# Running sums over sorted edges in a four-layer graph kernel: one-hot products replaced by scans over turned rows, and a straight-line GpSimd program

## The reference

```python
edge_index = jnp.stack([src, dst])
h = jnp.maximum(_layernorm(x), 0.0)
# GCN: segment sum by src of edge_weight * (h @ W)[dst]
x = x + segment_sum(edge_weight[:, None] * (h @ W)[dst], src) + bias
h = jnp.maximum(_layernorm(x), 0.0)
# GAT: x1 = leaky(h) @ W1.T + b1; hg = x1 @ Wg.T; 4 heads
alpha = leaky(a_src[src] + a_dst[dst], 0.2)          # per edge and head
coeff = softmax of alpha over the edges of one dst
x = x + leaky(segment_sum(hg[src] * coeff, dst) + bias_g, 0.01) @ W2.T + b2
h = jnp.maximum(_layernorm(x), 0.0)
# hypergraph: node -> hyperedge -> node
he = segment_sum((h * d_v_inv_sqrt)[src], dst_clipped) * (hw / d_e)
x = x + (segment_sum(he[dst_clipped], src) * d_v_inv_sqrt) @ W.T + b
h = jnp.maximum(_layernorm(x), 0.0)
# tensor product: weights per edge from a small network on edge_attr
mid = segment_sum(edge_features(h[src] @ w1, w(edge)), dst)   # 256 wide
x = x + linear(mid)
```

## Time and profile before

| what | value |
|---|---|
| median of 3 runs | 3786.72 us |
| lowest, highest | 3783.6, 3790.44 us |
| span of the profiled execution (its own time) | 4093.3 us |
| PE, PE weight loads | busy 48%, 37% of the span |
| DVE | 44% |
| ACT | 25% |
| POOL (GpSimd) | 68% |
| DMA, mean | 105 GB/s |

### The profile page before, as it was taken

One profiled execution on the slowest core, in us unless ns is written; L12 is line 12 of the kernel. 1 busy time (PEld: TensorE's weight loads), 2 busy tenths in 40 slices (PEclk: granted clock), 3 DMA queues, 4 the chain that ended last, 5 costly groups with the idle time before them and its releaser, 6 DMA issues.

```text
span 4093.3 us, 41473 instructions
## 1 busy us (share of the span) xinstructions
PE 1958.2 (48%) x8810; PEld 1502.6 (37%) x8810; DVE 1792.4 (44%) x5891; ACT 1029.1 (25%) x2706; POOL 2776.5 (68%) x2522
## 2 busy tenths in 40 slices
PE   0010002247731656557499923346666662216774
PEld 0000001135521444445377723334444441215773
DVE  2974301158831333233655426663333321207894
ACT  0000000134521444445011114442222221003442
POOL 0828876678886555553288876647888887667887
PEclk9999995567765666667555555555555555557997
DMA  3969813356652111111255434445555554437885
GB/s 86 307 116 332 282 36 97 95 116 106 109 84 46 39 39 42 39 39 25 41 69 69 62 58 116 120 112 104 102 102 102 95 98 99 115 101 156 171 171 104
DMA packets 469349, 430.13 MB, mean 105 GB/s; under 512 B 121817, under 2 KB 377975, under 8 KB 468979
## 3 DMA queue, kind: packets, MB, share of 16 engines
q0 software_dynamic: 156800, 133.81, 23.0%
q1 hardware_dynamic: 258098, 236.96, 18.5%
q10 hardware_dynamic: 54404, 58.86, 5.9%
HBM read 227.32 MB, written 148.92 MB: 92 GB/s over the span
## 4 chain that ended last, share of the span: by engine, by line
POOL 19%; issue 13%; DMA 6%; PE 4%; SPq 4%; DVE 2%; another core or an unknown queue 1%; ACT 1%; POOLq 0%; ACTq 0%; DVEq 0%
POOL out_dram L655 14%; POOL work L641 5%; DMA out_dram<-work 3%; DMA work<-big 2%; PE bank L806 1%; SPq L511 1%; PE bank L910 1%; PE bank L909 1%; SPq L504 1%; DMA work<-keys_clip 1%; POOL work L608 1%; ACT work L1124 1%; SPq L528 0%; SPq L145 0%
## 5 line engine op out<-in xcount | busy, mean ns | idle before, releaser
L655 POOL DMA_INDIRECT out_dram<-work x784 | 1258.5, 1605 | 268.2 <-issue 199.8
L641 POOL DMA_INDIRECT work<-out_dram,work x980 | 942.0, 961 | 613.1 <-issue 413.6
L806 PE MATMUL bank<-work 128*128 128x128 f32 x1568 | 378.1, 417 | 680.2 <-issue 316.4
L806 PEld LDWEIGHTS bank<-work 128*128 128x128 f32 x1568 | 334.1, 313 | 727.4 <-issue 568.4
L1669 DVE SCALAR_TENSOR_TENSOR work<-work,bank 128x128 f32<-128x128 f32 x975 | 320.5, 345 | 319.3 <-PE bank L806 183.3
L1124 ACT ACTIVATE work<-work 128x128 f32<-128x128 f32 x784 | 316.7, 480 | 128.7 <-issue 55.3
L641 POOL DMA_INDIRECT work<-rec_d,work x196 | 216.6, 1105 | 53.4 <-issue 46.7
L1652 DVE TENSOR_TENSOR work<-work 128x512 f32<-128x512 f32 x245 | 168.3, 687 | 175.7 <-DMA work<-keys_src 70.3
L641 POOL DMA_INDIRECT work<-he,work x196 | 199.9, 1020 | 53.6 <-issue 46.2
L853 PE MATMUL bank<-work,w_W1T 128*128 128x512 f32 x196 | 151.5, 917 | 118.0 <-ACT work L1187 108.9
L1117 ACT ACTIVATE work<-work,eps_col 128x4 f32<-128x4 f32 (+1 forms) x196 | 59.0, 301 | 549.1 <-issue 289.7
(11 more groups left out here) (281 smaller groups left out, 4400.5 us busy)
## 6 DMA issues: line engine op xcount, KB each, us to landing
out_dram<-big SPq DMA_DIRECT2D x71, 726.0 KB
big<-in_x_dram SPq DMA_DIRECT2D x71, 704.0 KB
work<-big SPq DMA_DIRECT2D x98, 264.0 KB
edge_w<-big SPq DMA_DIRECT2D x49, 512.0 KB
work<-edge_w ACTq DMA_DIRECT2D x49, 512.0 KB
work<-out_dram,work POOLq DMA_INDIRECT x980
big<-work SPq DMA_DIRECT2D x49, 264.0 KB
work<-keys_src ACTq DMA_DIRECT2D x49, 256.5 KB
```

The source lines that it names most:

```text
L641: g_.indirect_dma_start(ring_[G.place][:, k * columns:(k + 1) * columns], None, table_ap, bass.IndirectOffsetOnAxis(ap=idx_r[G.place][:, k ...
L655: g_.indirect_dma_start(table[:, :], bass.IndirectOffsetOnAxis(ap=idxa_r[G.place][:, k:k + 1], axis=0), ring_[G.place][:, k * ROW:(k + 1) ...
L806: last = T.matmul(out[:, t * P:(t + 1) * P], lhs[:, t * P:(t + 1) * P], rhs[:, t * P:(t + 1) * P], start=True, stop=True)
```

## The change

**Sums.** The one-hot product and the carry chain go. A flag per edge (1 where its key equals the key before it) is made once in stage 1 for each of the three key lists and stored in device memory; the key columns `key_col` for `clip` and `src` and the stored list `keys_clip` go. In each sum stage SP broadcasts 512 flags per group into a ring of 4 (`load_flags`), PE only transposes the rows (`turn_tiles`), and DVE makes one running scan over 512 edges per bank, state = flag * state + row, with the last column of the group before as its start. In GCN the transposing product has the edge weights on its diagonal (`diag`, made by ACT from `ident`).

**GpSimd.** All loops are written out (`every_group`); the gathers and adds take their indices from the index arrays where they lie; no index copies and no index DMAs. In GCN and TP the gathers write into `big` and the adds read from it; SP's copies, `big_in` and `fed` go. A gather of group G in these stages waits for the gathers of G-4 (`rows_in`), an add for `kept` of its group and the adds of G-4.

**GAT.** W1 and Wg, and W1 and the attention vectors, are multiplied together once in stage 1 (`WF`, `attF`, with the constant parts `bF4`, `att_c`); the steps `first` and `bias` go, and the buffers behind `turn` and `project` are doubled.

**HYP on DVE** is written in plain order (front, scan, scale), where before the carry chain was interleaved by hand with the statistics. `key_col` copies and a memset ahead of TP go; about 13 small DVE instructions and 4 matmuls are added to the preparation of the weights in stage 1.

```diff
-        def load_keys(eng, G, which, S):
-            if G.from_(2):
-                eng.wait_ge(S["sel"], G.g - 1)
-            k = keys_dram[which]
...
-            eng.dma_start(keys_r[G.slot][:, 0:GE + 1], part.partition_broadcast(P)).then_inc(keys_at.of(G), 16)
+        def load_flags(eng, G, which, S):
+            if G.from_(UNROLL):
+                eng.wait_ge(S["chained"], G.g - (UNROLL - 1))
+            k = flags_dram[which]
...
+            eng.dma_start(flag_r[G.place], part.partition_broadcast(P)).then_inc(flags_at.of(G), 16)
@@ SP
-            move_rows("GCN", GCN, ROW, idx["dst_s"], idx["add_s"])
+            for_groups(sp, lambda G: load_flags(sp, G, "src", GCN))
             stage_end(sp, 2)
-            for_groups(sp, lambda G: load_indices(G, "GAT", [idx["src_d"], idx["dst_d"]]))
...
-            move_rows("TP", TP, D, idx["src_d"], idx["add_d"])
+            for_groups(sp, lambda G: load_flags(sp, G, "dst", TP))
@@ GpSimd
             def gathers(name, table_ap, of, free=None, columns=ROW, ring_=rows_r, done_before=0):
-                def move(G):
+                def body(G):
                     if G.from_(UNROLL):
                         if free is None:
-                            big_in.wait(pool, name, G.before(UNROLL))
+                            rows_in.wait(pool, name, G.before(UNROLL))
                         else:
                             pool.wait_ge(free, G.g + (done_before - UNROLL + 1))
...
+                    for j, f in enumerate(of):
+                        for t in range(GROUP):
+                            k, at_ = j * GROUP + t, G.g * GROUP + t
+                            to = (big[:, at_ * ROW:(at_ + 1) * ROW] if free is None
+                                  else ring_[G.place][:, k * columns:(k + 1) * columns])
+                            g_.indirect_dma_start(to, None, table_ap,
+                                                  bass.IndirectOffsetOnAxis(ap=f[:, at_:at_ + 1], axis=0)
...
+            def adds(name, of, ready, ring_=None):
+                def body(G):
+                    pool.wait_ge(ready, G.g + 1)
+                    if G.from_(UNROLL):
+                        added.wait(pool, name, G.before(UNROLL))
...
+            def every_group(body):
+                for g in range(NG):
+                    body(group(g))
@@ PE
-            def sum_tiles(G, S, rhs, lhs, out, ready):
...
+            def turn_tiles(G, S, of, out):
+                if G.from_(2):
+                    pe.wait_ge(S["chained"], G.g - 1)
                 for t in range(GROUP):
+                    last = T.transpose(out[:, t * P:(t + 1) * P], of[:, t * P:(t + 1) * P], ident[:, :])
                 return last
@@ PE, GAT
+            def project(G):
...
+                T.matmul(b[:, :], one[0:1, :], bF4[0:1, :], start=True, stop=False)
                 for t in range(GROUP):
+                    T.matmul(b[:, t * P:(t + 1) * P], x_[:, t * P:(t + 1) * P], wts["WF"][:, :],
+                             start=False, stop=t == GROUP - 1)
@@ DVE
-            def carry_on(G, banks, ring_, t, k):
...
+            def run_scan(G, to, before, of, rows=slice(0, P)):
+                return V.tensor_tensor_scan(to, flag_r[G.place][rows, :], of, before if G.from_(1) else 0.0,
+                                            ALU.mult, ALU.add)
+            def chain(G, S, name, banks, ring_, free):
+                flags_at.wait(dve, name, G)
+                dve.wait_ge(S["turned"], G.g + 1)
                 if G.from_(2):
                     dve.wait_ge(S[free], G.g - 1)
+                if G.from_(1):
+                    dve.wait_ge(S["chained"], G.g)
+                for k, b in enumerate(banks):
+                    o = 512 * k
+                    ins = run_scan(G, ring_[G.slot][:, o:o + 512], ring_[1 - G.slot][:, o + 511:o + 512], b[:, :])
                 ins.then_inc(S["chained"], 1)
```

More of the change, by code:

```diff
@@ L313, in build_gnn @@
         added = Slots([sem(f"added{k}") for k in range(UNROLL)], [("GCN", 64), ("GATSUM", 64), ("HYPSUM", 64), ("TP", 64)])
[L314 to L321, removed]
+        flags_at = Slots([sem(f"flags_at{k}") for k in range(UNROLL)],
+                         [("GCN", 16), ("GATSUM", 16), ("HYP", 16), ("HYPSUM", 16), ("TP", 16)])
         def ring(start, size, n=2, dt=fp32):
@@ L871, in body @@
                 if G.from_(1):
-                    second(G.before())
-                first(G)
+                    project(G.before())
             for_groups(pe, body)
-            second(group(NG - 1))
+            project(group(NG - 1))
             stage_end(pe, 3)
@@ L934, in body, with turn @@
             def body(G):
[L935 removed]
+                turn(G)
                 if G.from_(1):
[L937 removed]
+                    back(G.before())
             for_groups(pe, body)
[L939 removed]
+            back(group(NG - 1))
             stage_end(pe, 6)
[L943 removed]
+            def turn(G):
                 rows_in.wait(pe, "HYPSUM", G)
[L945 removed]
+                turn_tiles(G, HYPSUM, rows_r[G.place], bank[G.slot]).then_inc(HYPSUM["turned"], 1)
             def delta(G):
@@ L1126, in norm @@
                 last.then_inc(S["h"], 1)
-            def next_keys(G, which, S):
-                if not (isinstance(G.g, int) and G.g == NG - 1):
-                    load_keys(act, G.after(), which, S)
             def keep(G):
@@ L1167, in keep @@
                 act.wait_ge(GAT["hh"], G.g + 1)
-                S_.copy(cols4(big, G, 512), bank[4][:, :]).then_inc(GAT["kept"], 1)
-            def bias(G):
-                act.wait_ge(GAT["xx"], G.g + 1)
-                for k in range(2):
-                    last = S_.activation(xxT8[:, k * 512:(k + 1) * 512], bank[2 + k][:, :], ACT.Identity, bias=cols[:, 0:1])
-                last.then_inc(GAT["xxs"], 1)
+                S_.copy(cols4(big, G, 512), bank[4 + G.slot][:, :]).then_inc(GAT["kept"], 1)
             def body(G):
@@ new lines, in front @@
+            def front(G):
+                rows_in.wait(dve, "HYP", G)
+                if G.from_(2):
+                    dve.wait_ge(HYP["turned"], G.g - 1)
+                r = rows_r[G.place].rearrange("p (t c) -> p t c", c=ROW)
+                V.tensor_tensor(t4(v_r[G.slot]), r[:, :, 0:D], over(wts["K2"][:, :], GROUP), ALU.subtract
+                                ).then_inc(HYP["taken"], 1)
+                dve.wait_ge(HYP["taken"], G.g + 1)
+                statistics(G, HYP, lambda t: v_r[G.slot][:, t * P:(t + 1) * P], GROUP)
```

453 lines of the change are left out of this document (150 added, 303 removed).

## The result

The changed kernel takes 3816.1 us (median of 4 runs, 3815.4 to 3817.0), the kernel before beside it 3785.2 us: a ratio of 1.0078, with a 95% interval of 1.0061 to 1.0096. It is slower by 31 us where 104 us less were forecast. In some groups of runs the kernel before takes 3785 us and in others 4054 to 4099 us, for reasons that stay open, so each ratio here is formed inside one group, and stage times are compared inside one kind of group.

What follows compares the result with a forecast made beforehand. POOL's issue without a gap was taken to bound every stage of an undisturbed execution. The terms -15 - 14 - 23 - 12 - 7 - 8 - 12 - 4 + 1 - 10 = -104 took 3787 to 3683 us; 8-in-10 range 3500 to 3745.

Steps and rivals of the forecast that it cites:

- Preparation: Stage 1: seventeen small DVE and PE instructions, three flag comparisons and stores, less index copies; +4 - 3 = +1 us.
- The choice of the basis: All terms taken against 3786.7 us, reading 304 us of POOL stalls as belonging to the profiled execution only.
- The first rival: Stalls where gathers run also exist in undisturbed executions, and the change cuts their chains: 3511 us, chance 0.15.
- Index copies in GATSUM: GATSUM's adds: without index copies in POOL's stream, adds at 1.595 us take 371.4 us in all; -15 us.
- HYP: HYP stage: gathers at 247 us, -14 us; separately its tail from 31.1 to 19 us, -12 us.
- GATSUM's first wait and GAT's tail: GATSUM's first add after 11 us instead of 18.67, -8; GAT's last group loses one product and one ACT pass, -4.
- Turns: GCN and TP, gathers to adds: without SP's copies the first add waits 4 us instead of 8.62 and 11.33; -12 us.
- Starts: Starts of GAT, GCN and TP: the index transfer behind the barrier goes, half of 5.03 us each; -7 us.
- Slots that DVE lengthens: POOL's gathers and adds lengthened by DVE's masks and carries: -10 us, bounds 0 and -42.
- Written-out loops: GpSimd's loops: 0.7 us for 10 jumps back in GCN's adds, so nothing to gain and nothing taken.
- At nothing, DVE's HYP body: DVE bodies counted as nothing, covered by POOL's issue, 5.0 us per group of gathers; the text names GCN's and TP's.
- The slower rival: Adds and gathers reading rows and indices in place make POOL's slots 0.146 us dearer: 3998 us, chance 0.06.

Runs made afterwards that it cites:

- Run 2: Kernel before with only a wait added: ACT takes no records until a DVE comparison behind its dense pass; 4216.8 against 4054.5 us, 1.039.
- run 3: Changed kernel again, 3815.5 us (1.0076), and beside it with the src flags' store behind the record copying, 3662.2 us (0.9672); before 3785.7.
- run 1: Changed kernel with ACT's store of the src flags moved behind the record copying, in a slower group; 3935.2 us against 4054.5 of before, 0.970.
- the moved store: Changed kernel with ACT's src flag store swapped behind the copying of records; 3935.2 us in a slower group, 3662.2 in a faster one.
- run 5: Kernel before with GpSimd's loops written out, indices read in place, no index copies or index DMAs; 3989.5 against 4054.5 us, 0.9843.
- run 6: As run 5, with GCN and TP gathering into the big buffer and SP's row copies gone; 3972.1 against 4054.5 us of before, 0.9792.
- its third run: Kernel of run 6 measured again in a slower group; 4002.8 us beside 4097.1 of before, 0.9772.
- run 7: The moved store with two two-input comparisons of 128x512 per group put back on DVE in all five sum stages; 3752.6 us, 90 more.
- run 8: The moved store with each scan of 128x512 made twice, one input in SBUF and one in PSUM; 3710.4 us, 48 more.

## Why the prediction was wrong

**The step that failed** is *Preparation*, priced at +1 us with its "three flag comparisons and stores"; it cost about 153. I counted what the stores cost and not what the third waits for. It stands in ACT's stream ahead of the copying of records, which it holds for DVE's whole dense pass. Run 2 gives the wait alone at 162 us, run 3 its removal at 153. The stage table shows it in one piece (434.7 against 282.6). The order of the instructions on ACT was to be had before the run; I looked at GpSimd's and DVE's alone.

**The choice of the basis** had a wrong reason, and did little harm. I took the 304 us of stalls for a thing of profiling, because they came to the same as the 306.6 us between span and median. But profiling does not make them: in run 1 the profiled execution took 3945.5 us with a span of 3943.3, in a group whose median is 3935.2, and its trace has them. They belong to the groups where before takes 4054 to 4099 us, and the 4093.3 us of the profiled execution of before lie among these. That before has none of them where it takes 3785 us is not shown, since no trace of it comes from such a group; the changed kernel has none there. In the timeline of the moved store in a slower group (run 1), GAT:

```profile
1545.71 1.95 PE L775 MATMUL bank<-ident,work 128*128 128x128 f32 x8
...
1559.04 1.07 ACT L1104 COPY work<-bank 128x512 f32<-128x512 f32 x2 [7.82 <-remote]
```

ACT copies the result of eight transposes 11 us after the end that the record gives them, as in the earlier trace rows. In the faster groups GAT's gathers take 490 to 492 us without a gap, 392 x 1.25, and in the slower ones 592 to 650. GCN shows it most. The windows from its first gather to its last, of the moved store in a slower group (run 1) and in a faster one (run 3), in the columns of the earlier trace rows:

```profile
575.40:828.50 253.10, 25.32 (x112) 20.96 (x112) 18.84 (x69) 16.16 (x46) 192.47 (x196) 0.56 0.25 59
...
578.20:824.60 246.40, 171.30 (x886) 133.82 (x887) 138.86 (x444) 106.45 (x319) 186.91 (x196) 0.74 0.36 88
```

In the slower one PE does 112 of its products beside the gathers, in the faster 886, in the same kernel; the rest is left for the adds. The first rival took the stalls for real and expected 82 + 112 us of them to be saved with the rest; in the slower groups the change without its wait gains 119 us (run 1), against 123.5 in the faster, and runs 5 and 6 show why it is no more: the stalls move from the gathers to the adds behind them. What makes the other engines late stays open.

**Term by term**, against the stage table and the runs:

- *Index copies in GATSUM*, -15: from 389.4 to 371.2 us, -18. The size is right and the cause only in part. Run 5, which takes the copies away and leaves the sums, has 381.5: 8 us for the copies. The other 10 came with the scans, as the mean add fell from 1.629 us in run 5 to 1.577. The sum took the adds at GCN's 1.595 and put all of the difference down to the copies.
- *HYP*, 247 us for the gathers and -12 in the tail: 247.1. The tail I can only compare inside the slower groups: 35.2 us from POOL's last gather to the next stage in run 6, 27.1 in run 1, -8.
- *GATSUM's first wait and GAT's tail*, -12: from GAT's last gather to GATSUM's first add 118.7 us in run 6 and 114.5 in run 1, -4; but the kernel of run 6 had 113.4 in its third run, so this one is not resolved. In the slower groups the tails were taken too high; for the faster ones nothing on record tells.
- *HYPSUM*, 629.7: 628.3 us.
- *Turns*, 4 us each: 2.5 and 2.5. *Starts*, -2.5 each: 2.6 to 2.8 us in place of 5.0 to 6.5. Both a little better.
- *Index loads, copies and turns together*, -71: runs 5 and 6 give -65 and -17, -82, in a slower group.
- *Slots that DVE lengthens*, -10 of at most -42: run 7 puts it at 46 us for two comparisons a group. I was too low. The sentence on the rule of the Trainium skill ("SBUF — State Buffer", "Who interferes with whom") gave -42, and here it was right: two inputs in SBUF lengthen GpSimd's slots (20 to 60 ns an add in run 7), and one does so by 13 ns at most (run 8).
- *Written-out loops*, 0: the trace bears no gain; but none was measured by itself, since run 5 changed the indices too. Nor does the loop's 0.7 us disagree with the rule of the Trainium skill cited there ("Runtime: NRT & Kernel Launch", "Instruction fetch mechanics"): it speaks of a jump out of the fetched window, and no run shows that this loop leaves it.
- *At nothing, DVE's HYP body*: right in the sum, wrong in the reason. Its cover is under one scan per group (runs 7 and 8).
- *The slower rival* named dearer slots as the mechanism. The kernel is slower, but its slots are cheaper than before or, in the gathers of GCN and GAT (0.960 and 0.951 us against 0.959 and 0.953), the same. The side was named with the wrong cause; what happened had no rival.
- *The case's own range*: without tails, turns and slots the sum gives 3729; its upper end of 3735 is not worked out.

## What to carry to other kernels

A new wait is priced by what stands behind it in the stream of the engine that waits, and by who needs that: here one DMA issue of 0.34 us cost 153 us. Look up the stream of every engine that the change touches, above all those with low shares, and ask of each new wait when its releaser runs. And when a span is longer than the median, the gap says that two executions differ, not that the profiler did it.

## What was not expected of the hardware

- A tensor_tensor of 128x128 on DVE took 0.29 us alone, and 2.3 to 3.3 us when it started within one of GpSimd's 128x1408 additions of 3.2 us. Giving GpSimd less of the work (10 chunks instead of 25) moved the end of the sort's steps from 292 to 250 us.
- An indirect add of 128 rows took 20 to 60 ns longer with two 2-input comparisons of 128x512 per group on DVE, and at most 13 ns with one more scan.
- A tensor_tensor_scan over 512 columns took 1.266 us, on one partition (1.267) as on 128.
- The kernel before took 3785 us in some groups and 4054 to 4099 us in others, and the kernel with the store moved 3662 and 3935 us. Of these 273 us, GAT with the softmax has 123 (706.0 against 583.3), HYP 72, GCN's adds 53 and TP's 23; the granted clock in GAT was 0.50 in both, and beside GCN's gathers PE did 112 products in the one and 886 in the other. What sets it is open.
